# A graph network layer in eight groups: another order for the first group, for the seams between groups and for the end

## The reference

```python
def gnn(x, mask, ...):                       # x: 32 graphs x 256 nodes x 128 features, float32
    xc = transpose(x)
    h = relu(bn1(conv1d(xc, conv1_w)))       # kernel width 1
    h = bn2(conv1d(h, conv2_w, pad=8))       # kernel width 17
    x_conv = transpose(relu(h + xc))
    s = x @ w_se.T + b_se                    # 3 features
    dist = sq[:, :, None] + sq[:, None, :] - 2 * s @ s.T
    A = exp(-dist) * mask                    # mask = adj here
    msg = relu(x @ w_msg.T + b_msg)
    x_nmp = A @ msg
    gi = [x_conv, x_nmp] @ w_ih.T + b_ih ; gh = x @ w_hh.T + b_hh
    r, z = sigmoid(...), sigmoid(...) ; n = tanh(gi_n + r * gh_n)
    return (1 - z) * n + z * x

x = layernorm(x + gnn(x, adj, ...))
h = (1 + eps) * x + adj @ x
x = layernorm(x + relu(h @ W1 + b1) @ W2 + b2)
```

## Time and profile before

| | us |
|---|---|
| median of 3 runs | 411.62 |
| lowest, highest | 411.33, 415.04 |
| the profiled execution | 411.75 |
| its span in the profile | 409.9 |

### The profile page before, as it was taken

One profiled execution on the slowest core, in us unless ns is written; L12 is line 12 of the kernel. 1 busy time (PEld: TensorE's weight loads), 2 busy tenths in 40 slices (PEclk: granted clock), 3 DMA queues, 4 the chain that ended last, 5 costly groups with the idle time before them and its releaser, 6 DMA issues.

```text
span 409.9 us, 6675 instructions
## 1 busy us (share of the span) xinstructions
PE 379.4 (93%) x2369; PEld 338.5 (83%) x2369; DVE 276.7 (68%) x552; ACT 235.8 (58%) x430; POOL 226.0 (55%) x215
## 2 busy tenths in 40 slices
PE   2679999999999999999999999999999999999873
PEld 1678889899898888899898988988888998988863
DVE  5688748867488647876588655876488665856563
ACT  3637466546755477446756377455766366553843
POOL 2616634947356645748248464657448483575342
PEclk9689999999999999999999999999999999999999
DMA  8302001201013010120012010130111110000101
GB/s 294 136 2 103 2 1 53 79 26 51 1 53 104 0 54 18 38 99 26 26 51 102 0 51 0 51 102 2 51 53 55 50 52 2 1 2 0 53 0 51
DMA packets 7559, 19.39 MB, mean 47 GB/s; under 512 B 624, under 2 KB 4976, under 8 KB 6384
## 3 DMA queue, kind: packets, MB, share of 16 engines
q1 hardware_dynamic: 7392, 19.02, 13.2%
q10 hardware_dynamic: 144, 0.07, 0.1%
HBM read 14.89 MB, written 4.19 MB: 47 GB/s over the span
## 4 chain that ended last, share of the span: by engine, by line
PE 57%; DVE 20%; issue 9%; ACT 6%; POOL 5%; DMA 2%; SPq 0%; DVEq 0%; ACTq 0%; POOLq 0%
PE back L1088 27%; PE conv L1088 12%; PE back L1250 6%; PE front L1163 6%; POOL rstd L474 4%; DVE xn L907 3%; DVE esum L852 3%; PE front L1135 2%; DVE usum L856 2%; DVE usum L840 2%; DMA tail<-in_conv_dram 2%; ACT tail L658 1%; DVE wl L939 1%; DVE stats L885 1%; DVE gbuf L871 1%
## 5 line engine op out<-in xcount | busy, mean ns | idle before, releaser
L1088 PE MATMUL conv<-sth,wh 128*128 128x256 f32 x320 | 99.1, 310 | 10.8 <-DVE stl L778 5.0
L1088 PE MATMUL conv<-stl,wh 128*128 128x256 f32 x320 | 93.0, 291 | 0.0
L1088 PE MATMUL conv<-sth,wl 128*128 128x256 f32 x320 | 92.9, 290 | 0.0
L1088 PEld LDWEIGHTS conv<-sth,wh 128*128 128x128 f32 x320 | 62.3, 195 | 14.5 <-DVE wl L939 8.4
L474 POOL TENSOR_TENSOR rstd<-rstd,minus_half 128x4 f32<-128x4 f32 (+1 forms) x34 | 36.1, 1062 | 65.7 <-DVE rstd L889 65.7
L1088 PEld LDWEIGHTS conv<-stl,wh 128*128 128x128 f32 x320 | 62.4, 195 | 1.0
L1088 PEld LDWEIGHTS conv<-sth,wl 128*128 128x128 f32 x320 | 62.2, 194 | 0.0
L479 POOL TENSOR_TENSOR xw<-xw,xv 128x512 f32<-128x512 f32 (+1 forms) x17 | 20.9, 1227 | 62.9 <-ACT xw L642 62.9
L492 POOL TENSOR_TENSOR amat<-amat,adjT 128x512 f32<-128x512 f32 x32 | 48.1, 1526 | 5.2 <-ACT amat L618 4.3
L649 ACT ACTIVATE xch<-usum 128x512 fp32r<-128x512 f32 x16 | 10.1, 632 | 35.9 <-DVE usum L856 35.9
L1163 PE MATMUL front<-amat,msg 128*128 128x256 f32 x128 | 30.2, 379 | 0.0
(11 more groups left out here) (199 smaller groups left out, 967.9 us busy)
## 6 DMA issues: line engine op xcount, KB each, us to landing
adjT<-in_adj_dram SPq DMA_DIRECT2D x8, 1024.0 KB, 4.8
out_dram<-tail SPq DMA_DIRECT2D x15, 256.0 KB, 2.2
xv<-in_x_dram SPq DMA_DIRECT2D x7, 512.0 KB, 3.3
tail<-in_conv_dram SPq DMA_DIRECT2D x1, 1088.0 KB, 6.2
gbuf<-in_gates_dram SPq DMA_DIRECT2D x1, 576.0 KB, 9.9
xv<-in_x_dram SPq DMA_DIRECT2D x2, 256.0 KB, 3.3
later_w<-in_later_dram SPq DMA_DIRECT2D x1, 452.0 KB, 6.9
out_dram<-tail SPq DMA_DIRECT2D x2, 128.0 KB, 1.7
```

Source lines behind the costliest of these rows:

```text
L1088: ins = pe.matmul(bank, a, b, start=first and k == 0, stop=last and k == len(todo) - 1)
```

## The change

What it does:

- The conv2 weights come in four transfers: two on SP's queue, two on ScalarE's queue ahead of `ident`. All users wait for all four. SP then waits for the weights and for x of group 0 before it issues x of group 1, adj of group 0 and the gates' weights, in that order.
- GpSimd makes `qsum` 5 to 8 and 10 to 13 and the low parts of the gates' weights and of W1 in place of VectorE; its masks, splits and differences are reordered around them.
- TensorE's first group: messages ahead of `taps(0, 0)`, factors after it, the four distances around `taps(0, 2)`, and both conv1 of group 1 ahead of `taps(0, 6)`, into two banks of the back (`ahead=True`); `taps(0, 8)` is no longer cut.
- ScalarE and VectorE follow that order.
- `pre_sum` is parted into `g_sum` and `pre_sum`. In `steady` `g_sum(gm, 1)` stands ahead of `diff_low(gf, 0)`, and `pre_sum(gm, 1)` ahead of the two `out_shift`.
- At the end, `out_norm(6, 0)` and `out_norm(6, 1)` move from ahead of the gates of group 7 to between them.

```diff
 # SP, prologue
-                sp.dma_start(c2raw, t["conv2"]).then_inc(conv2_loaded, 16)
+                sp.dma_start(c2raw[:, 0:5, :], t["conv2"][:, 0:5, :]).then_inc(conv2_loaded, 16)
+                sp.dma_start(c2raw[:, 5:9, :], t["conv2"][:, 5:9, :]).then_inc(conv2_loaded, 16)
                 sp.dma_start(later_w[:, :], t["later"]).then_inc(later_loaded, 16)
+                sp.wait_ge(conv2_loaded, 64)
+                wait(sp, X_LOADED, 0, 16)
+                load_x(1, 1)
                 load_adj(0, 0)
                 sp.dma_start(graw, t["gates"]).then_inc(gates_loaded, 16)
-                wait(sp, X_LOADED, 0, 16)
-                load_x(1, 1)
 # GpSimd, prologue
                 split_diff(0, 0)
+                pool.wait_ge(conv2_loaded, 64)
+                pool.tensor_tensor(qsum[:, 5:9, :], c2raw[:, 0:TAPS - 1:4, :], c2raw[:, 2:TAPS:4, :],
+                                   ALU.add).then_inc(tap_sums_ab, 1)
                 diff_a(0)
                 split_diff(0, 1)
+                pool.tensor_tensor(qsum[:, 10:14, :], c2raw[:, 1:TAPS:4, :], c2raw[:, 3:TAPS:4, :],
+                                   ALU.add).then_inc(tap_sums_ab, 1)
                 diff_b(0)
+                mask(0, 0, 0)
+                mask(0, 0, 1)
                 split_diff(0, 2)
-                for b in range(GB):
-                    mask(0, 0, b)
-                pool.wait_ge(bn_ready, 3)
+                mask(0, 0, 2)
+                mask(0, 0, 3)
                 split_diff(1, 0)
+                pool.wait_ge(w_high, 11)
+                pool.tensor_tensor(wl[:, S_GATE:S_GATE + 9, :], graw, full(wh[:, S_GATE:S_GATE + 9, :]),
+                                   ALU.subtract).then_inc(w_gate_low, 1)
+                pool.wait_ge(w_high, 12)
+                pool.tensor_tensor(w1l[:, :], w1raw, full(w1h[:, :]), ALU.subtract).then_inc(w_gate_low, 1)
                 diff_a(1)
                 split_diff(1, 1)
                 diff_b(1)
+                pool.wait_ge(bn_ready, 3)
 # ScalarE, prologue (after), from the first relu
+                act.dma_start(c2raw[:, 9:13, :], t["conv2"][:, 9:13, :]).then_inc(conv2_loaded, 16)
+                act.dma_start(c2raw[:, 13:TAPS, :], t["conv2"][:, 13:TAPS, :]).then_inc(conv2_loaded, 16)
                 act.dma_start(ident, t["consts"]).then_inc(consts_loaded, 16)
...
+                h1_out(0, 0); h1_out(0, 1); odd_high(0, 0); tap_high(0); tap_high(1); diff_high(0, 0)
+                tap_high(2); tap_high(3); odd_high(0, 1); factors_out(0); tap_high(4); tap_high(5)
+                mm_out(0); exps(0, 0); exps(0, 1); diff_high(0, 1); x_high(1, 1); exps(0, 2); exps(0, 3)
+                tap_high(6); tap_high(7); tap_high(8); odd_high(0, 2); am_out(0); msg_out(0, 0..2)
+                diff_high(0, 2); gates' high parts; h1_out(1, 0, True); h1_out(1, 1, True); odd_high(1, 0)
+                bm_out(0); W1's high part; xconv_high(0, 0); diff_high(1, 0); nmp_high(0, 0)
+                nmp_high(0, 1); xconv_high(0, 1)
 # VectorE, prologue (after), from the sums of taps
-                dve.tensor_tensor(qsum[:, 5:9, :], c2raw[:, 0:TAPS - 1:4, :], c2raw[:, 2:TAPS:4, :], ALU.add)
-                dve.tensor_tensor(qsum[:, 10:14, :], c2raw[:, 1:TAPS:4, :], c2raw[:, 3:TAPS:4, :], ALU.add).then_inc(tap_sums, 1)
+                messages(0, 0); tap_low(0); odd_low(0, 0); messages(0, 1); messages(0, 2); factors(0)
+                tap_low(1); diff_low(0, 0); tap_low(2); tap_low(3); odd_low(0, 1); tap_low(4); tap_low(5)
+                m_sum(0); diff_low(0, 1); x_low(1, 1, 0); x_low(1, 1, 1); tap_low(6); odd_low(0, 2)
+                tap_low(7); tap_low(8); diff_low(0, 2); x_sum(0, 0, 0); x_sum(0, 0, 1); g_sum(0, 0)
+                pre_sum(0, 0); odd_low(1, 0); diff_low(1, 0); nmp_low(0, 0); xconv_low(0, 0); diag
+                nmp_low(0, 1); g_sum(0, 1); pre_sum(0, 1); xconv_low(0, 1)
-                w_low_part(wl[:, S_GATE:S_GATE + 9, :], graw, wh[:, S_GATE:S_GATE + 9, :], 11)
-                w_low_part(w1l[:, :], w1raw, w1h[:, :], 12)
 # VectorE, steady
                     nmp_low(gm, 1)
+                    g_sum(gm, 1)
                     diff_low(gf, 0)
+                    pre_sum(gm, 1)
                     out_shift(gb, 0)
                     out_shift(gb, 1)
-                    pre_sum(gm, 1)
 # TensorE, prologue (after); each taps(0, n) still waits for its w_low
+                conv1(0, 0, 0); conv1(0, 0, 1); messages(0, 0); taps(0, 0); factors(0); taps(0, 1)
+                distances(0, 0); distances(0, 1); taps(0, 2); distances(0, 2); distances(0, 3)
+                taps(0, 3); taps(0, 4); taps(0, 5); conv1(1, 1, 0, True); conv1(1, 1, 1, True)
+                taps(0, 6); taps(0, 7); nmp(0, 0); taps(0, 8); nmp(0, 1); pe.wait_ge(w_gate_low, 2)
 # ScalarE, last
-                for h, c in LAST_ITEMS:
-                    gates(g, h, c)
+                gates(g, 0, WHOLE)
+                out_norm(g - 1, 0)
+                gates(g, 1, 0)
+                out_norm(g - 1, 1)
+                gates(g, 1, 1)
```

More of the change, by code:

```diff
@@ L280, in gnn_kernel @@
         w_low = sem("w_low")
+        w_gate_low = sem("w_gate_low")
+        tap_sums_ab = sem("tap_sums_ab")
         def wait(eng, name, g, j):
@@ L682, in prologue @@
                 h1_out(0, 0)
+                h1_out(0, 1)
+                odd_high(0, 0)
                 act.wait_ge(tap_sums, 1)
                 tap_high(0)
-                h1_out(0, 1)
-                odd_high(0, 0)
                 tap_high(1)
+                diff_high(0, 0)
                 tap_high(2)
-                diff_high(0, 0)
-                act.wait_ge(tap_sums, 2)
+                act.wait_ge(tap_sums_ab, 1)
                 tap_high(3)
+                odd_high(0, 1)
+                factors_out(0)
                 tap_high(4)
+                tap_high(5)
                 mm_out(0)
-                tap_high(5)
-                odd_high(0, 1)
+                exps(0, 0)
+                exps(0, 1)
                 diff_high(0, 1)
-                for k in range(3):
-                    msg_out(0, k)
+                x_high(1, 1)
+                exps(0, 2)
+                exps(0, 3)
+                act.wait_ge(tap_sums_ab, 2)
                 tap_high(6)
@@ L841, in x_sum, with g_sum @@
                                        by_graph(esum[:, :, :]), ALU.add), U_READY)
-            def pre_sum(g, par):
+            def g_sum(g, par):
                 if par == 0:
@@ L973, in prologue @@
                 dve.tensor_tensor(qsum[:, 0:4, :], msum[:, 0:NM - 1:2, :], msum[:, 1:NM:2, :], ALU.add).then_inc(tap_sums, 1)
-                dve.tensor_tensor(qsum[:, 5:9, :], c2raw[:, 0:TAPS - 1:4, :], c2raw[:, 2:TAPS:4, :], ALU.add)
-                dve.tensor_tensor(qsum[:, 10:14, :], c2raw[:, 1:TAPS:4, :], c2raw[:, 3:TAPS:4, :], ALU.add).then_inc(tap_sums, 1)
+                dve.wait_ge(later_loaded, 16)
+                dve.wait_ge(factors_set, 2)
+                messages(0, 0)
                 tap_low(0)
                 odd_low(0, 0)
+                messages(0, 1)
+                messages(0, 2)
+                factors(0)
                 tap_low(1)
+                diff_low(0, 0)
                 tap_low(2)
[L980 to L985, removed]
                 tap_low(3)
+                odd_low(0, 1)
                 tap_low(4)
                 tap_low(5)
-                odd_low(0, 1)
+                m_sum(0)
                 diff_low(0, 1)
-                m_sum(0)
+                x_low(1, 1, 0)
+                x_low(1, 1, 1)
                 tap_low(6)
+                odd_low(0, 2)
                 tap_low(7)
                 tap_low(8)
-                odd_low(0, 2)
                 diff_low(0, 2)
@@ L998, in prologue @@
                 x_sum(0, 0, 1)
+                g_sum(0, 0)
                 pre_sum(0, 0)
[L1000 to L1004 removed]
+                odd_low(1, 0)
+                diff_low(1, 0)
+                nmp_low(0, 0)
                 xconv_low(0, 0)
[L1006 to L1007 removed]
+                dve.wait_ge(consts_loaded, 16)
+                dve.scalar_tensor_tensor(diag[:, :], ident, vec[:, EPS1:EPS1 + 1], ident,
+                                         ALU.mult, ALU.add).then_inc(bn_ready, 1)
                 nmp_low(0, 1)
[L1009 removed]
+                g_sum(0, 1)
                 pre_sum(0, 1)
@@ L1032, in steady @@
                 x_sum(gm, u, 1)
+                g_sum(gm, 0)
                 pre_sum(gm, 0)
@@ L1117, in taps, with conv1 @@
                     done(ins, CONV_FULL[n])
-            def conv1(g, u, h):
-                wait(pe, G_READY, g - 1, 1) if h == 0 else wait(pe, BMS_READY, g - 1, 1)
+            def conv1(g, u, h, ahead=False):
+                if not ahead:
+                    wait(pe, G_READY, g - 1, 1) if h == 0 else wait(pe, BMS_READY, g - 1, 1)
                 wait(pe, XL_READY, g, h + 1)
```

(9 more changed lines are left out.)

59 lines of the change are left out of this document (28 added, 31 removed).

## The result

| | us |
|---|---|
| changed kernel, median of 14 runs | 409.91 |
| lowest, highest | 408.45, 411.52 |
| kernel before, median of 14 runs beside it | 412.20 |
| ratio | 0.9939, 95% interval 0.9917 to 0.9960 |
| profiled execution, its span | 410.32, 408.5 |

The change made the kernel 2.3 us faster, 0.6%. The forecast was 407.0 us, 4.7 us faster, so about half of the forecast gain came. The measured time lies inside the stated range, and the gain is within the 1% that the prediction counted as no change. The two profiles differ by 1.4 us of span. Their parts are larger than their sum, and two of them are losses.

The account below looks back on a forecast made before the run. TensorE's work was taken to bound the middle groups, with VectorE and GpSimd taking turns at the start. First group 2.2, seams 2.4 and end 0.1 sum to 4.7 off 411.75: 407.0 us, range 401.5 to 410.5.

Parts of the forecast that it names:

- The sum: Whole kernel: first group 2.2, seams 2.4 and end 0.1 us add to 4.7 us won, giving 407.0 us.
- the second rival: Start and end: half clock behind TensorE's new holes makes the kernel slower, 414.5 us with two falls; chance 0.07.
- a clock under 1.00 after 45 us: TensorE's granted clock: named as a sign that the forecast is wrong.
- The first group: Start of the kernel: taps(1, 1) near 45.6 us against 47.80, a gain of 2.2 us.
- The walk through the two queues: First group: VectorE and GpSimd operations taken by turns put taps(1, 1) near 46.0 us, 45.6 with the weights sooner.
- the delay of x: Start, SP's queue: x and adj issued some 5 us later, costed at nothing.
- The bound of -1 to 8 us: First group's gain: 7.9 if turns seldom meet, about -1 if GpSimd's 2.8 us subtraction comes during VectorE's x sums.
- 6.1 us of shared time: First group: 2,432 new elements hold GpSimd, and with it the pair, 6.1 us; VectorE is relieved of about 2.5.
- the 7.9 given as the most: First group: 7.9 us gained were TensorE the only limit, up to 10 with another half-clock stretch gone.
- The third rival: First group: the port shared by VectorE and GpSimd eats its whole gain; 409.3 us, range 408.5 to 411; chance 0.18.
- The seams: Between groups: TensorE's six waits for line 852 go, 2.4 us won, bounds 1.5 and 2.4.
- The first rival: First group: TensorE is its bound, giving 5 to 8 us there; 401.2 to 404.2 us in all; chance 0.27.

Follow-up runs that it names:

- e2: Kernel before with the end part alone, out_norm of group 6 between the gates of group 7: 414.49 us, ratio 1.0060 to the kernel before.
- e5: Changed kernel with 16 extra, never-read products on TensorE between taps(1, 0) and taps(1, 1): 409.46 us, ratio 0.9926 to the kernel before.
- e8: Changed kernel with the low parts of the gates' weights and W1 back on VectorE, behind group 0's x sums: 409.24 us, 0.9921 of the kernel before.
- e9: Changed kernel with the low parts of the gates' weights and W1 at the end of VectorE's prologue: 407.15 us, 0.9877 of the kernel before.
- e6: Changed kernel with 28 extra products in the hole ahead of the last group's last transposes: 408.09 us, ratio 0.9902 to the kernel before.
- e3: Changed kernel with the steady seams and the end as before, so the first group's part alone: 411.20 us, ratio 0.9975 to the kernel before.
- e1: Kernel before with the seam part alone, g_sum ahead of diff_low and out_shift behind pre_sum: 408.99 us, ratio 0.9922 to the kernel before.
- e13: Changed kernel, gates' and W1's low parts late on VectorE, extra products ahead of taps(0, 7) and the last transposes, both tap sums back on VectorE: 403.43 us, 0.9771.
- e10: Changed kernel with the gates' and W1's low parts at the end of VectorE's prologue and the old end: 407.17 us, 0.9844 of the kernel before.
- e4: Changed kernel with the old end, out_norm of group 6 ahead of the gates of group 7: 408.78 us, 0.9925 of the kernel before.
- e11: Changed kernel, gates' and W1's low parts at the end of VectorE's prologue, 28 extra products ahead of the last transposes: 405.41 us, 0.9813 of the kernel before.

## Why the prediction was wrong

**The step that failed is the price of the longer hole at the end.** The sum put the end at 0.1 won; alone it lost 2.3 (e2). The account stood in the second rival. It named the mechanism, the place and the length: a hole of 3.9 us at the end, and holes of 2 to 2.5 ahead of `taps(0, 7)` and `taps(1, 1)`. It gave it 0.07, because it tied the falls to a sign and to a first group that wins less than 2.7 us. The falls were then left out of the sum, where they belonged: the fall at the end was in every profile with a hole of 3.85 to 3.87 us and no extra products (after, e2, e5, e8, e9). e2 prices it at 2.3 us, e6 at 1.5 to 1.8. With it, the forecast would have been 2.4 to 3.2 us. That this comes near the 2.3 measured is partly luck, since two further errors partly cancel: the first group was forecast 1.2 too high and the seams 0.8 too low. The prediction had also named a clock under 1.00 after 45 us as a sign against itself, and both falls, at 48 and at 389 us, are such.

**The first group.** Forecast 2.2, in the profile 1.17, alone (e3) 1.0, between 0 and 2.1. The walk through the two queues had the right form: operations that take turns, `g_sum` last, `taps(1, 1)` near 46 (46.39 to 47.13 in the profiles that keep the changed kernel's first group as it is). What the forecast got wrong first is the place that it measured from. The 47.80 is one execution, in which half clock followed the hole of 2.79 us. e1 and e2 keep the old first group, and in their profiles it did not follow. TensorE's timelines of e1, then e2:

```profile
15.27 0.55 PE L1095 MATMUL conv<-sth,wh 128*128 128x256 f32 x1 [6.45 <-DVE stl L778]
...
47.14 0.35 PE L1095 MATMUL conv<-sth,wh 128*128 128x256 f32 x1 [0.70 <-DVE esum L852]
```

```profile
14.69 0.55 PE L1092 MATMUL conv<-sth,wh 128*128 128x256 f32 x1 [5.91 <-DVE stl L782]
...
46.63 0.36 PE L1092 MATMUL conv<-sth,wh 128*128 128x256 f32 x1 [0.70 <-DVE esum L856]
```

e2's `taps(1, 1)` starts at 46.63, where the changed kernel's does. From the first taps to `taps(1, 1)` are 34.28 us in the kernel before, 31.87 in e1, 31.94 in e2 and 31.89 in the changed kernel. So against executions of the old order without that fall the new first group wins next to nothing. That the 1.0 of e3 comes from executions in which the fall is avoided fits this, but no run shows it.

The second error is the cost of the delay of x, which I had put at nothing. The first product of the kernel starts at 5.88 to 5.92 in the three profiles with the old start and at 6.78 to 7.57 with the new one. The two halves of x took 4.6 us to land in the median, before 3.3, while two transfers of weights on ScalarE's queue were under way; that these were the cause is likely, and no run parts it. VectorE's sums of taps then began at 8.18, behind VectorE's own queue:

```profile
8.18 1.22 DVE L991 TENSOR_TENSOR gbuf<-tail 128x1024 f32<-128x1024 f32 x1
```

That is only 0.2 us sooner than in the profile of the kernel before (8.40). But there the time varies with the landing of the weights: with the old start the sums waited for them until 10.15 in e1 and 9.57 in e2, with the new one they began between 8.18 and 9.32 and in no profile waited for them. The 1.2 us by which the first taps are later than in the profile before are no mean loss either: 14.69 and 15.27 in e2 and e1, 14.51 to 15.23 with the changed kernel's first group. The bound of -1 to 8 us held.

**The moved work.** The forecast charged it 6.1 us of shared time against 2.5 won on VectorE and still took the order as it was. e8 shows that the move of the low parts won nothing, e9 and e13 that the whole move cost time against making the same parts where VectorE idles: with it undone the first group wins another 4.0 us (46.63 to 42.65), half of the 7.9 given as the most. The Trainium skill's sentence in "Perfetto Trace Analysis", "Optimizing Scalar/DVE Operations", that such a move "might not help", held: here it cost.

**The third rival** (the shared port eats the whole first part, 409.3) was nearest to the time, 409.91, and partly right in its reason: the first part gave about 1.0 us in the mean (0 to 2.1), little or nothing without the fall of the clock, and 4.0 more once the moved work was taken off GpSimd. That its time fits is luck as well, because the seams gave more than its 2.4 and the end lost what it left out.

**The seams.** Forecast 2.4 with 2.4 as the upper bound, measured 3.2 twice, in the profiles and in e1. The order of events was as forecast; the size was not. The idle time that a row shows ahead of TensorE's instruction is counted from the modelled end of the one before: at the seam shown, the last product starts at 94.33, the next at 94.95, 0.62 later, where products follow each other after 0.12. The loss is 0.50, not 0.34.

**The end.** On ScalarE 0.2 for 0.1. On TensorE as above.

**The first rival** (TensorE as the bound, 0.27) fell: TensorE waits for VectorE at both new holes, and VectorE was busy 41.0 of the first 47.8 us after, 35.5 before. `taps(1, 1)` starts no earlier than 46.39 in any profile of this first group, where that rival needs 38 to 41.

## What to carry to other kernels

Work moved from VectorE to GpSimd cost time in this kernel wherever VectorE had operations with two SBUF operands to make beside it. Look at how long a VectorE operation beside the moved one takes (2.83 us here for one of 0.69), and first look for a stretch where VectorE idles. When a change makes TensorE finish sooner but something else still ends last, write down the length of the hole that opens, and put the half clock behind it into the sum; a few idle products in the hole are a cheap test and, here, the cure. Before a hole or a fall of the clock in one profile goes into a sum, look whether it is in a second execution of the same code: the 47.80 was not. Value a wait of TensorE by the distance between the starts of the two instructions, not by the idle time shown.

## What the runs showed of the hardware

The same hole costs clock in one execution and not in another. 2.79 us ahead of `taps(0, 3)` was followed by half clock in the profile of the kernel before; in e1's profile the same hole was not, as the first product's 0.36 us against 0.55 shows (TensorE's timeline of e1):

```profile
27.11 0.36 PE L1095 MATMUL conv<-sth,wh 128*128 128x256 f32 x1 [2.78 <-DVE wl L941]
```

Holes of 2.52 and 2.53 us at the end were followed by half clock in e3 and e10, and not in the kernel before, e1 and e4. Holes of 2.29 to 2.31 ahead of `taps(0, 7)` were followed by it in eight profiles and not in e11's. Holes of 1.6 to 2.0 ahead of `taps(1, 1)` were followed by it in the changed kernel and not in e3, e4, e6 and e8. Those of 3.85 to 3.87 were in all five profiles that have one. Part of this kernel's spread goes with the clock: e1 lay between 407.17 us at a mean clock of 0.994 and 411.58 at 0.974 and 0.982, while e13 lay between 403.08 and 404.45, at 0.995 to 0.998. Not all of it does: e3 has 412.37 us at 0.994 and 410.39 at 0.990. The landing of the weights, after which the sums of taps could start at 8.40, 9.57 or 10.15 us with the same code, is another part. And the mean clock can miss a slow stretch: in e1's profile the first 15 products of the taps run at half clock, with starts 0.21 us apart up to 18.40, while the column shows 1.00 from 13 to 21 us. What decides whether half clock follows a hole of 1.6 to 2.8 us is not settled by these runs.
